# Attention in a decoder layer: full-row score products, weighing groups spread over the steps, two evacuations apart

## The reference

```python
scores = jnp.einsum('nhbqd,nhbkd->nhbqk', qb, kb) / math.sqrt(d)   # window: keys of block -64 .. +192
probs = softmax(scores); ctx = jnp.einsum('nhbqk,nhbkd->nhbqd', probs, vb)
idx = bos, the 62 tokens with the largest |q|, eos                 # per head
g_scores = jnp.einsum('nhqd,nhkd->nhqk', qg, k) / math.sqrt(d)     # these see all keys
ctx = ctx.at[bn, bh, idx].set(softmax(g_scores) @ v)
```

## Time and profile before

| | us |
|---|---|
| median of three runs (lowest, highest) | 1193.27 (1190.8, 1193.4) |
| the profiled execution, its time | 1194.69 |
| its span | 1193.0 |

### The profile page before, as it was taken

One profiled execution on the slowest core, in us unless ns is written; L12 is line 12 of the kernel. 1 busy time (PEld: TensorE's weight loads), 2 busy tenths in 40 slices (PEclk: granted clock), 3 DMA queues, 4 the chain that ended last, 5 costly groups with the idle time before them and its releaser, 6 DMA issues. The chain is left out here.

```text
span 1193.0 us, 16414 instructions
## 1 busy us (share of the span) xinstructions
PE 1033.2 (87%) x4682; PEld 653.1 (55%) x4683; DVE 548.6 (46%) x1171; ACT 442.6 (37%) x762; POOL 424.7 (36%) x423
## 2 busy tenths in 40 slices
PE   5999995899999999925999999927899999999960
PEld 4557883444443443314888889914456556555530
DVE  3325435776777777208788888620111111111104
ACT  3332210567667676624444444301112212212114
POOL 2000000255465464445566666312223233233224
PEclk9999997799999999956999999967989999999985
DMA  7454306234244242042111111107973333343327
GB/s 244 154 186 159 141 1 129 55 82 106 68 90 105 55 104 54 1 132 84 54 54 54 54 53 53 45 10 255 269 198 61 63 70 57 66 69 55 70 36 282
DMA packets 80876, 115.66 MB, mean 97 GB/s; under 512 B 15680, under 2 KB 37056, under 8 KB 80832
## 3 DMA queue, kind: packets, MB, share of 16 engines
q1 hardware_dynamic: 65648, 90.17, 26.0%
q0 software_dynamic: 9760, 20.49, 9.5%
q10 hardware_dynamic: 5424, 4.46, 1.2%
HBM read 74.77 MB, written 40.31 MB: 96 GB/s over the span
## 5 line engine op out<-in xcount | busy, mean ns | idle before, releaser
L553 POOL TENSOR_TENSOR pair_sum<-probs 128x2048 f32<-128x2048 f32 x32 | 146.1, 4565 | 164.1 <-ACT probs L692 164.1
L717 DVE TENSOR_REDUCE maxima<-ps_s 128x8 f32<-128x512 f32 x256 | 168.6, 689 | 71.4 <-PE ps_s L585 69.6
L692 ACT ACTIVATE probs<-ps_st 128x512 f32<-128x512 f32 x256 | 146.6, 600 | 93.1 <-PE ps_st L634 89.6
L1532 POOL DMA_INDIRECT x_dram<-e_y,who x39 | 62.1, 1593 | 215.0 <-ACT e_y L1557 211.1
L585 PE MATMUL ps_s<-k,q 96*128 96x512 f32 x256 | 115.4, 458 | 14.7 <-DMA k<-qk_dram 11.8
L634 PE MATMUL ps_st<-q,k 128*128 128x512 f32 x256 | 121.2, 475 | 4.8 <-ACT probs L692 2.5
L1583 DVE COPY e_gT<-e_ps_gT 128x384 f32<-128x384 f32 x39 | 21.7, 557 | 215.0 <-PE e_ps_gT L1622 215.0
L634 PEld LDWEIGHTS ps_st<-q,k 128*128 128x128 f32 x256 | 49.2, 193 | 109.7 <-ACT probs L692 77.0
L1614 PE MATMUL e_ps_g<-w_all,xgT 128*128 x312 | 106.7, 487 | 2.7 <-DMA w_all<-in_L_ffn_w_down_dram 2.0
L1630 PE MATMUL e_ps_y<-w_all,e_gT 128*128 (+1 forms) x234 | 107.0, 593 | 0.8 <-DVE e_gT L1583 0.8
L1614 PE MATMUL e_ps_u<-w_all,xgT 128*128 x312 | 99.0, 460 | 0.0
(11 more groups left out here) (224 smaller groups left out, 1851.3 us busy)
## 6 DMA issues: line engine op xcount, KB each, us to landing
qk_dram<-qk_ctx SPq DMA_DIRECT2D x32, 512.0 KB, 2.8
q<-qk_dram SPq DMA_DIRECT2D x96, 128.0 KB
k<-qk_dram SPq DMA_DIRECT2D x96, 128.0 KB
w_all<-in_L_ffn_w_gate_dram SPq DMA_DIRECT2D x8, 704.0 KB
w_all<-in_L_ffn_w_up_dram SPq DMA_DIRECT2D x8, 704.0 KB
x_dram<-x SPq DMA_DIRECT2D x16, 256.0 KB, 2.1
x_dram<-attn SPq DMA_DIRECT2D x16, 256.0 KB
w_all<-in_L_ffn_w_down_dram SPq DMA_DIRECT2D x8, 512.0 KB
```

The lines of the kernel that those rows point to most:

```text
L553: pool.tensor_tensor(pair_sum[:, h], probs[:, 2 * h], probs[:, 2 * h + 1], ALU.add).then_inc(added, 1)
L692: act.activation(probs[:, kc, j, :], ps_st[:, s % 2, :], ACT.Exp, scale=SCALE).then_inc(exp_done, 1)
L717: dve.tensor_reduce(by_tile[:, t, j, 1:9], ps_s[:, x % 2, :].rearrange("p (g n) -> p g n", n=S // 8), axis=AX.X, op=ALU.max).then_inc(s_re ...
L1532: pool.indirect_dma_start(out=x3_dram[:], out_offset=bass.IndirectOffsetOnAxis(ap=who[:, j, 0:1], axis=0), in_=y[:, p, :], in_offset=None, ...
```

## The change

It has six parts, all in `attend`.

- The score product takes all 128 rows. For this, rows 96 to 127 of `q4` are zeroed by one more transfer for each unit, at the head of its load, from a zeroed tile `no_shift`, which VectorE clears at the start of the stage and for which SP waits. NDMA grows to 16 x 13.
- EARLY goes from 5 to 6: scores 6 to 15 of unit u+1 at steps 0 to 9, scores 0 to 5 of unit u+2 at steps 10 to 15.
- TensorE's groups move: weighings of this unit to steps 5, 10 and 13, the second sums of the unit before to step 8, its way back to 12, the turn to 13, behind the weighing.
- ScalarE's two evacuations part: the output after exponential 2, the sums after exponential 10, each with a semaphore. Shift copies go after exponentials 13 (one), 14 (two) and 15 (one).
- VectorE takes the maxima of scores 0 and 1 of unit u+2 before the division, those of 2 to 5 behind it.
- GpSimd copies the values first, then makes the second pair sum of the unit before, then the first of this one.

```diff
-NDMA = 16 * 12
+NDMA = 16 * 13
-EARLY = 5
+EARLY = 6
...
                     pool.tensor_copy(vu[:].rearrange("p t d -> p (t d)"), slot(c.v, u)).then_inc(v_in, 1)
-                    for h in range(2):
-                        pool.wait_ge(exp_done, NU * u + 2 * HPG * (h + 1))
-                        need(pool, sums_done, 2 * (u - 1) + h + 1)
-                        pool.tensor_tensor(pair_sum[:, h], probs[:, 2 * h], probs[:, 2 * h + 1], ALU.add).then_inc(added, 1)
+                    if not (isinstance(u, int) and u == 0):
+                        add(u - 1, 1)
+                    add(u, 0)
+                    if is_last(u):
+                        add(u, 1)
...
+                    sp.dma_start(q4[BR:P, p].bitcast(F32),
+                                 no_shift[:].bitcast(F32).rearrange("p (a n) -> p a n", a=1).to_broadcast([HD, HPG, S])).then_inc(unit_in[p], 16)
...
+                sp.wait_ge(zero_done, 1)
...
-                    pe.matmul(ps_s[:, x % 2, :], q4[0:BR, p, j, t * P:(t + 1) * P], k4[0:BR, p, j, :],
+                    pe.matmul(ps_s[:, x % 2, :], q4[:, p, j, t * P:(t + 1) * P], k4[:, p, j, :],
...
-                            if s == 7:
+                            if s == 8:
                                 sums(u - 1, 1)
-                            if s == 10:
+                            if s == 12:
                                 back(u - 1)
-                        if s in (11, 12, 13):
-                            weigh(u, s - 11)
-                        if s == 14 and not last:
+                        if s in (5, 10, 13):
+                            weigh(u, (5, 10, 13).index(s))
+                        if s == 13 and not last:
                             turn(u + 1)
...
-                def evacuate(u):
+                def take_o(u):
                     act.wait_ge(pv_done, TT * u + TT)
+                    act.wait_ge(backed, u + 1)
+                    act.activation(outT[:], ps_o[:], ACT.Copy).then_inc(o_taken, 1)
+
+                def take_sum(u):
                     act.wait_ge(sums_done, 2 * u + 2)
-                    act.wait_ge(backed, u + 1)
-                    act.activation(outT[:], ps_o[:], ACT.Copy).then_inc(evacuated, 1)
-                    act.activation(sumT[:], ps_sum[:], ACT.Copy).then_inc(evacuated, 1)
+                    act.activation(sumT[:], ps_sum[:], ACT.Copy).then_inc(sum_taken, 1)
...
-                        if s == 8 and not first:
-                            evacuate(u - 1)
-                        if s >= 14 and not last:
-                            for j in range(2):
-                                take_shift(u + 1, (p + 1) % SLOTS, 2 * (s - 14) + j)
+                        if s == 2 and not first:
+                            take_o(u - 1)
+                        if s == 10 and not first:
+                            take_sum(u - 1)
+                        if s >= 13 and not last:
+                            for j in ((0,), (1, 2), (3,))[s - 13]:
+                                take_shift(u + 1, (p + 1) % SLOTS, j)
...
+                    ahead = not (isinstance(u, int) and u > U - 3)
+                    if ahead:
+                        for x in range(2):
+                            reduce(u + 2, x)
                     if not first:
                         normalise(u - 1)
-                    if not (isinstance(u, int) and u > U - 3):
-                        for x in range(EARLY):
+                    if ahead:
+                        for x in range(2, EARLY):
                             reduce(u + 2, x)
...
+                dve.memset(no_shift[:].bitcast(F32), 0.0).then_inc(zero_done, 1)
```

More of the change, by code:

```diff
@@ L485, in attend @@
         vu = m.sb("vu", [P, TT, P])
+        no_shift = m.sb("no_shift", [HD, S], F32R)
         ones = m.sb("ones_sum", [P, HD])
@@ L512, in attend @@
         pv_done, added, sums_done = m.sem("pv_done"), m.sem("added"), m.sem("sums_done")
-        evacuated, backed, recip_done, normed = m.sem("evacuated"), m.sem("backed"), m.sem("recip_done"), m.sem("normed")
+        backed, recip_done, normed = m.sem("backed"), m.sem("recip_done"), m.sem("normed")
         row_step, turn_ready, turned, shift_ready = m.sem("row_step"), m.sem("turn_ready"), m.sem("turned"), m.sem("shift_ready")
         cleared, window_in = m.sem("cleared"), m.sem("window_in")
+        o_taken, sum_taken, zero_done = m.sem("o_taken"), m.sem("sum_taken"), m.sem("zero_done")
         def slot(t, u):
@@ L549, in unit, with add @@
                     pool.tensor_copy(vu[:].rearrange("p t d -> p (t d)"), slot(c.v, u)).then_inc(v_in, 1)
-                    for h in range(2):
-                        pool.wait_ge(exp_done, NU * u + 2 * HPG * (h + 1))
-                        need(pool, sums_done, 2 * (u - 1) + h + 1)
-                        pool.tensor_tensor(pair_sum[:, h], probs[:, 2 * h], probs[:, 2 * h + 1], ALU.add).then_inc(added, 1)
+                    if not (isinstance(u, int) and u == 0):
[3 more added lines that the diff above has]
+                        add(u, 1)
+                def add(u, h):
+                    pool.wait_ge(exp_done, NU * u + 2 * HPG * (h + 1))
+                    need(pool, sums_done, 2 * (u - 1) + h + 1)
+                    pool.tensor_tensor(pair_sum[:, h], probs[:, 2 * h], probs[:, 2 * h + 1], ALU.add).then_inc(added, 1)
                 units(pool, unit)
@@ L601, in weigh @@
                         pe.wait_ge(v_in, u + 1)
-                        need(pe, evacuated, 2 * u)
+                        need(pe, o_taken, u)
                     for j in range(HPG):
@@ L611, in sums @@
                     if h == 0:
-                        need(pe, evacuated, 2 * u)
+                        need(pe, sum_taken, u)
                     for j in range(HPG):
@@ L618, in back @@
                 def back(u):
-                    pe.wait_ge(evacuated, 2 * u + 2)
+                    pe.wait_ge(o_taken, u + 1)
+                    pe.wait_ge(sum_taken, u + 1)
                     pe.wait_ge(normed, u + 1)
@@ L692, in unit @@
                         act.activation(probs[:, kc, j, :], ps_st[:, s % 2, :], ACT.Exp, scale=SCALE).then_inc(exp_done, 1)
-                        if s == 8 and not first:
-                            evacuate(u - 1)
-                        if s >= 14 and not last:
-                            for j in range(2):
-                                take_shift(u + 1, (p + 1) % SLOTS, 2 * (s - 14) + j)
+                        if s == 2 and not first:
[5 more added lines that the diff above has]
+                                take_shift(u + 1, (p + 1) % SLOTS, j)
                     if last:
-                        evacuate(u)
+                        take_o(u)
+                        take_sum(u)
                 for j in range(HPG):
```

## The result

The changed kernel takes 1242.95 us (median of four runs, 1238.9 to 1243.64) against 1192.03 for the kernel before (four runs): a ratio of 1.042, 95% interval 1.040 to 1.044. It is 51 us slower; 24 were forecast (1217 us, range 1203 to 1233). The profiled execution took 1238.9 us, the shortest of the four; its span is 1237.1.

A forecast was written before the change was run, and what follows sets the result against it. TensorE's order of work, held up by other engines, was taken as the bound. Unit: floor 16.2 plus waits 3.4 = 19.6 us, +1.4; over the stage +19, load +1.7, clock +3 on 1193.3: 1217 us, range 1203 to 1233.

The forecast's parts named there:

- the stall: Step 12, ahead of the way back: TensorE's score x=2 waits 1.5 us a unit behind VectorE's row maxima; ends 1.0 and 1.8.
- The floor, 16.2 us: One unit on TensorE: plain steps, six groups, transposes and way back without waits take 16.2 us, unchanged by the edit.
- the waits at the unit's start and at steps 4 to 8: TensorE waits for exponentials, maxima and shift copies: 0.7 us at the start, 1.2 at steps 4, 5 and 8.
- Row maxima ... 2.06 us.: VectorE, after the maxima of score 15: row maxima take 2.06 us, counted as 2.1 in the chain to score x=2.
- A few of fourteen stretches ... I take two, +3.: Clock after a wait and the way back: two falls to half clock, +3 us; ends 0 and, with eight, +14.
- the rival with eight falls and more: The clock falls in most units, eight times or more: 1228 to 1240 us; chance 0.12.
- The first load, +1.7: First unit's load: zeroing transfer 1.2 us and SP's wait for VectorE's clearing about 0.5, once; ends +0.5 and +2.5.
- the prologue, +0.6: Ahead of the loop: one more score is made, +0.6 us once.
- Evacuations apart, -0.9: Way back at step 12: sums are evacuated at step 10, so its 0.9 us wait goes to 0.
- The full rows, 0: Score products on 128 instead of 96 rows: no change taken in a unit, ends 0 and -0.3 us.
- 96 rows cost drains: Rival: 96-row score products drain TensorE, so full rows save up to 1.8 us a unit: 1190 to 1203 us; chance 0.07.
- The spread wins: Rival: no wait at score x=2, 1192 to 1195 us, or 1165 if ScalarE's order costs nothing; chance 0.13 for both.

The follow-up runs named there:

- pair sum behind the maxima: Changed kernel with GpSimd starting a unit's first pair sum only after VectorE has finished the row maxima: 1206.31 us, ratio 1.012 to the kernel before.
- new order: Kernel before (96 rows, EARLY = 5) with TensorE's groups, the two evacuations and VectorE's division moved to other places: 1171.46 us, ratio 0.981.
- filled kernel: Changed kernel with seven products, results overwritten, in the wait ahead of the score at step 12: 1224.98 us, ratio 1.027 to the kernel before.
- rows alone: Kernel before with the score product on all 128 rows and the zeroing transfer, order unchanged: 1195.45 us, ratio 1.002.
- one score later: Changed kernel with EARLY back at 5, turn at step 14, shift copies two and two after steps 14 and 15: 1195.23 us, ratio 1.002 to the kernel before.

## Why the prediction was wrong

The direction was right, and the stall stands at the step that the prediction named and for the reason that it gave. Two terms of the sum failed: the row maxima, whose time was taken over from the old order, and the falls of the clock, which are the larger miss (17 us in the profile where 3 were taken).

- *The floor, 16.2 us, and the waits at the unit's start and at steps 4 to 8.* They fit: the changed unit without the wait on GpSimd takes 19.1 us (pair sum behind the maxima), and its score at step 12 starts 1.33 us behind the product before it, 1.1 more than the 0.24 without a wait. That is about the 1.5 less the 0.5 that GpSimd had held there before. Other steps fit as they stood: the product of step 1 starts 1.23 us behind that of step 0 (0.58 in the new order, where nothing waits, so 0.65; forecast 0.7).
- *"Row maxima ... 2.06 us."* This is the step that failed first. I took the time between two rows of VectorE for VectorE's work. 0.5 of it was a wait for GpSimd, and a wait does not move with its instruction: the row maxima start 0.7 us sooner behind the start of the pair sum, which still ends when it ends, so the chain takes 2.8 us, 0.7 more than before, where 2.06 was carried over. That is 0.7 a unit, nine over the stage, and it puts the stall (2.2) outside the ends that were given for it (1.0 and 1.8). The price list had "GpSimd" only for who waits for its result, not for what it holds up while it runs.
- *"A few of fourteen stretches ... I take two, +3."* Ten falls, 17 us in the profile, 18 by the filled kernel. The stretch that I compared with had waits of 0.45 and 0.48 ahead of the way back, the new one has 2.15 in one piece; the rival with eight falls and more (chance 0.12) was what happened, and the time lies above even its 1240. The two misses are one chain: with the stall of 1.1 us no fall is left in the steady units and with products in the stall none is left either.
- *The first load, +1.7, and the prologue, +0.6.* About right: some 2 us by the start of the first score, 3 by the time of the rows alone (0 to 5 by its interval), and 0.6 from the first score to the first transposed product. The sum had nothing for the first unit, which takes 3.0 more: its score at step 12 waits 2.72 us instead of 0.81 one step later, and a fall follows.
- *Evacuations apart, -0.9.* The wait went, as said, and in the changed kernel the stall takes its place. Alone, with the sums at step 8, it gained nothing: what it won at the way back was lost at steps 5 and 13, the first of which the prediction had priced (0.45) for its own order.
- *The full rows, 0.* Right for the products (0.03 a unit at most), and the drains of the rival are not there; that fewer falls go with this part was not foreseen.
- *Rivals.* "96 rows cost drains" is out (rows alone). "The spread wins" is out with the stall that its condition excluded; one score later shows that the spread together with the parted evacuations and GpSimd's order is worth next to nothing in a unit. The spread was not run by itself.

The sum with the terms as the two profiles show them: 13 units of 2.13 make 28, the falls 17, the first unit 3, load and prologue 1.7, the last two units -4, the stages behind -1: 44 to 45 us, against 44 between these two executions and 51 between the medians.

Open: how the clock decides. What was shown is that the falls stand at the stall, that products in the stall or a shorter stall stop them in the steady units, and that without the full rows and their transfer there were more of them. Open also: how much of the loss the turn's place makes by itself, and which of the moves of the new order gives what.

## What to carry to other kernels

In a hand-written order, follow each product that is made ahead back to what frees its buffer, and add up that chain against the work that stands between; moving a product one step earlier, ahead of a long group, can put a whole chain on the path. Before a duration is carried over to another order, compare the same instruction's least and median duration and look at what the other engines end at that moment: here a small instruction that took four times its least was waiting. A stall on TensorE costs its length and then perhaps the clock behind it, so price both.

## What was not expected of the hardware

- A VectorE sum of 128 x 16 elements from two SBUF inputs takes 0.175 us when no pair sum runs and is held until GpSimd's running pair sum ends: 0.65, 1.38 and 2.44 us in the profiles. The maxima, one input from PSUM, keep their 0.68 to 0.70 us in the whole stage.
- Cutting the GpSimd instruction in four does not free VectorE: each two-input instruction in turn can be caught, 0.62 and 1.20 us.
- The clock fell in ten of fourteen units with a stall of 2 to 2.7 us, near its end, for 3.4 or 6.8 us each; 1.7 us of products whose results are not used, in each unit but the first, kept it up and made the kernel 18 us faster.
- With zeros on the 32 added rows, and the transfer that brings them, falls were fewer (ten against fourteen in one profile each, and a higher granted clock in four executions each) although nothing more is computed.
